# Cross-attention by token class and a mixture-of-experts layer on one core: the second norm's use and the scatter one round later, the front and routing pass one in another order, and unused small products on PE

## The chip, the cores and the metric

The kernel runs on one core of one Trainium2 chip. The metric is the device time of one execution in microseconds (us). Engines: PE (TensorE, matrix products), DVE (VectorE), ACT (ScalarE), POOL (GpSimd), and SP (SyncE), which issues DMAs.

## What is computed

The input x has 2048 tokens of 512 float32 features. The reference, cut to what matters:

```python
# first layer: each token belongs to one of 4 classes by its id; ctx is (4, 512, 512)
h = layernorm(x)
y = (silu(h @ ctx[e].T) * (h @ ctx[e].T)) @ ctx[e].T      # e = class of the token
x = x + y
# second layer
g = layernorm(x); n = rmsnorm(g) * norm_w
scores = softmax(n @ gate_w.T)                            # 32 experts, the 4 best per token, weights normed
routed = sum over the 4: weight * ((silu(n @ w13[e][:, :256]) * (n @ w13[e][:, 256:])) @ w2[e])
shared = (silu(n @ sg) * (n @ su)) @ sd
out = x + g + routed + shared
```

## The kernel before, in words

All large products are done in three parts: each float32 operand is split in a high part (rounded to fp32r, by ACT) and a low part (the difference, by DVE), and PE adds high x high, high x low and low x high (`three_products`, lines 221 to 223). Work goes by tiles of 128 tokens.

**First stage (`context`).** Tokens are sorted by class with a table made of one-hot products; here they fill 18 tiles, each of one class. One class's matrix (`ctx`, 512 x 512) is split by `high(e)` on ACT (line 476) and `low(e)` on DVE (line 536, about 2.3 us each). Each engine then runs a software pipeline written by hand: `pipeline` takes a list of parts with skews, and in round i it emits the parts in the order of the list, part p for tile i - skew(p). Rounds 0 to 11 are unrolled, with the tile's number known, then follows a loop. The order in the list is the order in the engine's queue, so a wait holds up all that stands behind it. The parts of a tile:

- POOL `gather` (skew 0, line 374): indirect DMA of the tile's rows of x; `rstd1` (2, lines 379, 381, 384): the first norm's scale and bias; `rstd2` (7, lines 391 to 398): those of the second norm (`affine`); `scatter` (9, line 406): indirect DMA of the results `hb` to `hb_dram`. Order: scatter, rstd1, rstd2, gather.
- DVE `stats1` (2, lines 612, 615): statistics of the rows; `x1` (7, lines 641, 644, 647): the residual sum and its statistics, which waits for base of the tile two before, as x1 has two buffers; `t1lo` (3, line 630), `t2lo` (5, line 634): low parts; `rows` (8, line 624): the scatter's index; `hn` (8, line 653); `weights` (0): low(1) in round 3, low(2) and low(3) in round 4, and pieces of the shared weights; `a` (4, line 627): the product with the gate.
- ACT `t1hi` (3, line 506), `t2hi` (5, line 510), `keep` (2, line 498), `weights` (0), `h` (2, line 515), `silu` (4, line 502), `x2` (7, line 520), `base` (8, line 525), in this order.
- PE `t1` (3) and `t2` (5), four transposes each (line 440); `g1` (4) and `g2` (6), twelve products each. Order: t1, t2, g1, g2.

h, a, x1, x2 and `hb` have two buffers. `rows`, `hn` and `base` of a tile wait until the scatter of the tile two before has landed. When all scatters have landed, POOL raises `stored`, and SP reads the first four tiles of the second stage (line 332).

**Second stage (`shared_routing_and_experts`).** Routing pass one goes over 8 pairs of tiles: PE transposes them (line 848), ACT and DVE split them (lines 977 and 1074), PE makes the logits (into `sps_gu`), ACT copies them (`lrow`, line 985), PE turns them back (`back`, line 864), DVE subtracts the maximum (`shift`, lines 1056, 1057), ACT takes exp (line 981), DVE finds the best (`top`, lines 1063 to 1066). On DVE round q is shift(q-2), t1lo of the pair q, top(q-3); on ACT it is t1hi of pair q, exp(q-2), lrow(q-1); on PE t1 of pair q, logits(q-1), back(q-2). SP refills the four row buffers (line 763). Then come the tables of the second sort (DVE, up to line 1213, which raises `listed`), beside the shared expert (PE, lines 221 to 223; POOL adds its results to `out`, line 800), and the experts: 80 tiles, gathered (lines 794, 822), run through PE and added to `out` by line 836, while the experts' weights stream in and are split (lines 1041 and 1253).

Of the kernel before, what the change touches and what calls it, by code (L numbers as in the profile page):

```python
# [22 lines left out]
ACT = mybir.ActivationFunctionType  # L23
AX = mybir.AxisListType

P = 128
# [3 lines left out]
G = TOKENS // P  # L30
# [23 lines left out]
RMS_EPS = 1e-6  # L54
W_SETS = 3
HL = C + CI


class Memory:
# [131 lines left out]
def number_of_quads(eng, entry):  # L191

    return eng.value_load(entry, min_val=0, max_val=MAX2 // RING - MIN_QUADS) + MIN_QUADS
# [11 lines left out]
def looked_up(eng, row, back, base, found):  # L205

    def look(pair):
        v = eng.value_load(row[:, bass.ds(pair, 1)], min_val=0, max_val=base ** (back + 1) - 1)
        for i in range(back + 1):
            found[i - back] = (v // base ** i) % base  # L210
    return look
# [7 lines left out]
def three_products(pe, acc, left_hi, left_lo, right_hi, right_lo, start, stop):  # L219

    pe.matmul(acc, left_hi, right_hi, start=start, stop=False)  # L221
    pe.matmul(acc, left_hi, right_lo, start=False, stop=False)  # L222
    return pe.matmul(acc, left_lo, right_hi, start=False, stop=stop)  # L223


def build(nc, m):
# [22 lines left out]
def context(nc, m):  # L249


    with ExitStack() as st:
# [82 lines left out]
        def _(pool):  # L335
# [71 lines left out]
                                            hb[:, t.par].rearrange("p a n -> p (a n)"), None,  # L407
                                            bounds_check=TOKENS - 1, oob_is_err=False).then_inc(hbs[t.par], 16)

            pipeline(pool, pairs, [("scatter", 9), ("rstd1", 2), ("rstd2", 7), ("gather", 0)], emit)  # L410
            m.carry(pool)
            count = number_of_pairs(pool, m.tab1[0:1, 1, 0:1], MAX1)
            for q in hbs:
# [3 lines left out]
        @block.tensor  # L417
        def _(pe):
            pe.wait_ge(m.s["consts"], 1)
            pe.wait_ge(m.s["counted"], 1)  # L420
            for g in range(G):
                mm = pe.matmul(ps_cnt, m.ones_b[:], M[:, g, :], start=(g == 0), stop=(g == G - 1))
            mm.then_inc(m.s["counts"], 1)
            pe.matmul(ps_rank, m.before_b[:], M[:].rearrange("p g e -> p (g e)"), start=True, stop=False, skip_group_check=True)
            for g in range(1, G):
                mm = pe.matmul(ps_rank[:, g * E1:], m.ones_b[:], M[:, 0:G - g].rearrange("p g e -> p (g e)"), start=False,
                               stop=(g == G - 1), skip_group_check=True)
            mm.then_inc(m.s["ranked"], 1)
            for i in range(G):
                pe.wait_ge(m.s["onehot"], i // C + 1)  # L430
                mm = pe.matmul(ps_list, hot[:, i, 0:P], hot[:, i, P:P + MAX1], start=(i == 0), stop=(i == G - 1))
            mm.then_inc(m.s["table"], 1)
            pe.wait_ge(m.s["listed"], 2)
            pairs = number_of_pairs(pe, m.tab1[0:1, 1, 0:1], MAX1)

            expert = {}

            def turn(dst, src):
                for c in range(C):
                    mm = pe.transpose(dst[:, c * P:(c + 1) * P], src[:, c * P:(c + 1) * P], m.ident[:])  # L440
                return mm

            def product(dst, hi, lo, t):
                e = bass.ds(expert[t.off], 1)
                for c in range(C):
                    mm = three_products(pe, dst[:], hi[:, t.par, c], lo[:, t.par, c], m.cth[:, e, c, :], m.ctl[:, e, c, :],
                                        c == 0, c == C - 1)
                return mm

            def emit(part, t):  # L450
                if part == "t1":
                    pe.wait_ge(s["h"], t.n + 1)
                    wait(pe, s["t1lo"], t.n)
                    turn(ps_t1, h[:, t.par]).then_inc(s["t1"], 1)
                elif part == "g1":
                    pe.wait_ge(m.s["ctx_split"], expert[t.off] + 1)
                    pe.wait_ge(s["t1lo"], t.n + 1)
                    wait(pe, s["a"], t.n)
                    product(ps_z, hth, htl, t).then_inc(s["g1"], 1)
                elif part == "t2":  # L460
                    pe.wait_ge(s["a"], t.n + 1)
                    wait(pe, s["t2lo"], t.n)
                    turn(ps_t2, a[:, t.par]).then_inc(s["t2"], 1)
                elif part == "g2":
                    pe.wait_ge(s["t2lo"], t.n + 1)
                    wait(pe, s["x1"], t.n - 1)
                    product(ps_y[t.par], ath, atl, t).then_inc(s["g2"], 1)

            pipeline(pe, pairs, [("t1", 3), ("t2", 5), ("g1", 4), ("g2", 6)], emit,
                     looked_up(pe, m.tab1[0:1, 0, :], BACK1, E1, expert))  # L470

        @block.scalar
        def _(act):
            def high(e):
                act.wait_ge(m.s[f"ctx_loaded{e}"], 16)
                nc.scalar.activation(m.cth[:, e], craw[:, e], ACT.Copy).then_inc(m.s["ctx_hi"], 1)

            high(0)
            act.wait_ge(m.s["gate_loaded"], 16)
            nc.scalar.activation(m.ghl[:, :, 0:E2], graw[:], ACT.Copy).then_inc(m.s["gate_hi"], 1)  # L480
# [44 lines left out]
                    nc.scalar.activation(hb[:, t.par, 1], x1[:, t.par], ACT.Identity, bias=affine[:, t.par, 1:2],  # L525
                                         scale=affine[:, t.par, 0:1]).then_inc(s["base"], 1)

            pipeline(act, pairs, [("t1hi", 3), ("t2hi", 5), ("keep", 2), ("weights", 0), ("h", 2), ("silu", 4), ("x2", 7), ("base", 8)], emit)

        @block.vector  # L530
        def _(dve):
# [63 lines left out]
            k(dve.tensor_scalar(tbf[:, 1, 0:1], row[0:1, 4, E1 - 1:E1], float(1 - 2 * MIN_PAIRS), None, ALU.add))  # L595
            k(dve.tensor_copy(m.tab1[:, 1, 0:1], tbf[:, 1, 0:1]))
            dve.tensor_scalar(m.tab1[:, 1, 0:1], m.tab1[:, 1, 0:1], 1, None, ALU.logical_shift_right).then_inc(m.s["listed"], 1)
            dve.wait_ge(m.s["listed"], 2)
            pairs = number_of_pairs(dve, m.tab1[0:1, 1, 0:1], MAX1)

            def emit(part, t):
                if part == "weights":
                    if isinstance(t.n, int):
                        for e in {3: (1,), 4: (2, 3)}.get(t.n, ()):
                            low(e)
                        if SHARED <= t.n < SHARED + HL // 2:
                            dve.wait_ge(m.s["sh_hi"], t.n - SHARED + 1)
                            dve.tensor_tensor(m.wl_s[:, piece(t.n)], sraw[:, piece(t.n)], m.wh_s[:, piece(t.n)].bitcast(F32),
                                              ALU.subtract).then_inc(m.s["sh_lo"], 1)
# [42 lines left out]
                    wait(dve, hbs[t.par], 16 * t.half)  # L652
                    dve.tensor_tensor(hb[:, t.par, 0], x2[:, t.par], m.normw[:], ALU.mult).then_inc(s["hn"], 1)

            pipeline(dve, pairs, [("stats1", 2), ("index", 0), ("x1", 7), ("t1lo", 3), ("t2lo", 5), ("rows", 8), ("hn", 8), ("weights", 0), ("a", 4)], emit)


def hots_of(i):
# [5 lines left out]
def shared_routing_and_experts(nc, m):  # L664


    with ExitStack() as st:
# [177 lines left out]
        def _(pe):  # L845
# [88 lines left out]

            pe.wait_ge(e["listed"], 1)
            pe.wait_ge(s["w_lo"], 2 * PIECES)
            quads = number_of_quads(pe, m.tab2[0:1, 2, 0:1])

            expert = {}
# [30 lines left out]

        @block.scalar
        def _(act):
            for q in range(G // 2 + 2):
                if q < G // 2:
                    for i in (2 * q, 2 * q + 1):
                        act.wait_ge(s["t1"], i + 1)
                        nc.scalar.activation(turned_hi(i).rearrange("p c n -> p (c n)"), turned[i % RING][:], ACT.Copy).then_inc(s["t1hi"], 1)
                if q >= 2:
                    act.wait_ge(s["shifted"], q - 1)
                    wait(act, s["top"], q - 3)  # L980
                    nc.scalar.activation(prob[:, q % 2], logits[:, q % 2], ACT.Exp).then_inc(s["exp"], 1)
                if 1 <= q <= G // 2:
                    act.wait_ge(s["logits"], q)
                    wait(act, s["back"], q - 2)
                    nc.scalar.activation(lraw[:, (q - 1) % 2], ps_gu[(q - 1) % 2][0:E2, 0:2 * P], ACT.Copy).then_inc(s["lrow"], 1)

            for i in range(G + 2):
                if i < G:
                    act.wait_ge(s["g1"], i + 1)
# [58 lines left out]
        def _(dve):  # L1048
# [5 lines left out]
            def shift(q):  # L1054
                dve.wait_ge(s["back"], q + 1)
                k_(dve.tensor_reduce(red[:, 2 * q:2 * q + 2], logit[q % 2], AX.X, ALU.max))
                dve.tensor_tensor(logits[:, q % 2], logit[q % 2], red[:, 2 * q:2 * q + 2].rearrange("p (j o) -> p j o", o=1).to_broadcast([P, 2, E2]),
                                  ALU.subtract).then_inc(s["shifted"], 1)

# [5 lines left out]
                dve.max_index(idx8[:, 2 * q, :], top8[:, 2 * q, :], prob[:, q % 2, 0])  # L1065
                dve.max_index(idx8[:, 2 * q + 1, :], top8[:, 2 * q + 1, :], prob[:, q % 2, 1]).then_inc(s["top"], 1)

            for q in range(G // 2 + 3):
                if 2 <= q < G // 2 + 2:
                    shift(q - 2)  # L1070
                if q < G // 2:
                    for i in (2 * q, 2 * q + 1):
                        dve.wait_ge(s["t1hi"], i + 1)
                        dve.tensor_tensor(turned_lo(i).rearrange("p c n -> p (c n)"), turned[i % RING][:],
                                          turned_hi(i).rearrange("p c n -> p (c n)").bitcast(F32), ALU.subtract).then_inc(s["t1lo"], 1)
                if q >= 3:
                    top(q - 3)
            dve.wait_ge(s["top"], G // 2)

            def low_a(i):  # L1080
# [203 lines left out]
```

## Time and profile before

| | us |
|---|---|
| median of 3 runs | 725.7 |
| lowest and highest run | 723.7, 728.16 |
| the profiled execution | 724.31 |
| its span, first to last instruction | 722.6 |
| PE busy in it | 629.1 (87%) |
| DVE, ACT, POOL busy | 440.7, 366.4, 339.4 |
| first stage, to the first read of the second | 0 to 184.6 |
| routing pass one, tables and shared expert, experts | to 221, to 304, to the end |

Times in the text are positions in the profiled execution, from the span's start. The time of an execution is a little longer than its span. Matrix products are pipelined on PE and the ends of the rows are modelled: the distance between two starts is the better measure of one. In brackets stands how long the engine was idle before a row and what released it; "issue" is time in which it waited for nothing that the profile shows. PEclk is the granted TensorE clock, 1.00 at full speed (2.4 GHz) and 0.50 at half (1.2 GHz).

### The profile page before, as it was taken

The numbers are of one execution on the slowest core, as the hardware profiler recorded it, in microseconds if no ns is written. First come the engines' busy times: TensorE is split into PE (matmuls) and PEld (weight loads), VectorE is DVE, ScalarE is ACT, GpSimd is POOL, SyncE is SP. The second block draws the span as 40 slices with busy tenths as digits, with TensorE's granted clock in tenths as the row PEclk, the third lists the DMA queues.
The fourth block names the chain that finished last, engine by engine and source line by source line (L and its number), as shares of the span: only waits on it lengthen the run. The fifth ranks groups of instructions, "written<-read, shape, count | busy, mean of one in ns | idle before, by whom it ended". The sixth has DMA issues, their size and how long they took to land.

```text
span 722.6 us, 15076 instructions
## 1 busy us (share of the span) xinstructions
PE 629.1 (87%) x3144; PEld 506.8 (70%) x3145; DVE 440.7 (61%) x1021; ACT 366.4 (51%) x635; POOL 339.4 (47%) x373
## 2 busy tenths in 40 slices
PE   2379998991579999889999999999999999999990
PEld 2268766771457788668887888788788788787870
DVE  7548666753268999745556556666554765655630
ACT  4357656542332422245566556666554665656530
POOL 2536676644000111245445464745665475565532
PEclk9989999997699999999999999999999999999996
DMA  6511222212676465466878888998787897978555
GB/s 240 171 39 61 99 88 87 108 67 87 195 271 212 59 142 120 60 158 194 218 214 234 211 239 234 260 286 209 196 254 213 239 252 233 243 228 232 115 64 69
DMA packets 35789, 124.68 MB, mean 173 GB/s; under 512 B 4784, under 2 KB 5936, under 8 KB 31152
## 3 DMA queue, kind: packets, MB, share of 16 engines
q0 software_dynamic: 24256, 59.26, 37.6%
q1 hardware_dynamic: 11504, 65.09, 25.2%
q8 instruction: 12, 0.20, 0.1%
q14 instruction: 17, 0.14, 0.1%
HBM read 90.51 MB, written 39.06 MB: 179 GB/s over the span
## 4 chain that ended last, share of the span: by engine, by line
PE 41%; DMA 21%; issue 12%; POOL 9%; DVE 8%; ACT 4%; POOLq 2%; ACTq 1%; DVEq 1%; SPq 0%
DMA out<-r_oh,e_sidx 10%; PE sps_gu L221 7%; PE sps_gu L223 7%; PE sps_gu L222 7%; DMA out<-normw,e_sidx 4%; PE sps_t L221 3%; PE sps_t L223 3%; PE sps_t L222 2%; DMA out<-r_rank,e_sidx 2%; POOL hb_dram L406 2%; DMA raw<-in_experts_w 1%; DMA both<-in_x,gather 1%; POOL c_rs L394 1%; POOL c_rs L381 1%; PE sps_table L848 1%
## 5 line engine op out<-in xcount | busy, mean ns | idle before, releaser
L1253 DVE TENSOR_TENSOR wl<-raw,wh x87 | 105.8, 1226 | 54.9 <-ACT wh L1041 51.2
L221 PE MATMUL sps_gu<-wh,s_xth 128*128 x320 | 133.0, 416 | 3.2 <-DVE s_xtl L1236 3.1
L223 PE MATMUL sps_gu<-wh,s_xtl 128*128 x320 | 126.6, 396 | 0.0
L222 PE MATMUL sps_gu<-wl,s_xth 128*128 x320 | 125.7, 393 | 0.0
L836 POOL DMA_INDIRECT out<-r_oh,e_sidx x40 | 68.0, 1700 | 88.8 <-issue 65.4
L1041 ACT ACTIVATE wh<-raw x87 | 91.2, 1060 | 16.0 <-issue 8.1
L822 POOL DMA_INDIRECT both<-hb_dram,e_gidx x76 | 81.7, 1074 | 32.2 <-issue 18.0
L221 PEld LDWEIGHTS sps_gu<-wh,s_xth 128*128 128x128 f32 x320 | 60.6, 189 | 15.3 <-issue 5.1
L1016 ACT ACTIVATE both<-sps_gu 128x256 f32<-128x256 f32 x80 | 30.6, 383 | 78.0 <-PE sps_gu L223 77.8
L223 PEld LDWEIGHTS sps_gu<-wh,s_xtl 128*128 128x128 f32 x320 | 60.5, 189 | 13.8
L221 PE MATMUL sps_t<-wh,s_ath 128*128 x160 | 69.6, 435 | 0.4
L222 PEld LDWEIGHTS sps_gu<-wl,s_xth 128*128 128x128 f32 x320 | 60.8, 190 | 10.7
L800 POOL DMA_DIRECT2D out<-both x16 | 14.1, 882 | 110.3 <-ACT both L1004 110.3
L223 PE MATMUL sps_t<-wh,s_atl 128*128 x160 | 63.0, 394 | 0.0
L222 PE MATMUL sps_t<-wl,s_ath 128*128 x160 | 62.7, 392 | 0.0
L1233 DVE TENSOR_TENSOR both<-both,sps_gu 128x256 f32<-128x256 f32 x80 | 33.4, 417 | 43.1 <-ACT both L1016 42.1
L836 POOL DMA_INDIRECT out<-normw,e_sidx x20 | 36.7, 1833 | 35.2 <-DMA out<-r_oh,e_sidx 31.6
L1236 DVE TENSOR_TENSOR s_xtl<-sps_rank,s_xth 128x512 fp32r<-128x512 f32 x40 | 27.5, 687 | 32.1 <-ACT s_xth L1020 32.1
L836 POOL DMA_INDIRECT out<-r_rank,e_sidx x20 | 33.3, 1663 | 24.4 <-DMA out<-normw,e_sidx 9.4
L1028 ACT ACTIVATE r_oh<-sps_t,weight 128x512 f32<-128x512 f32 x40 | 27.4, 684 | 30.1 <-PE sps_t L223 19.3
L1236 DVE TENSOR_TENSOR s_xtl<-sps_cols,s_xth 128x512 fp32r<-128x512 f32 x40 | 27.6, 689 | 18.5 <-ACT s_xth L1020 18.5
L223 PEld LDWEIGHTS sps_t<-wh,s_atl 128*128 128x128 f32 x160 | 30.0, 188 | 6.8
(300 smaller groups left out, 1426.0 us busy)
## 6 DMA issues: line engine op xcount, KB each, us to landing
raw<-in_experts_w SPq DMA_DIRECT2D x32, 1536.0 KB, 7.8
craw<-in_ctx_w SPq DMA_DIRECT2D x4, 1024.0 KB, 7.6
both<-hb_dram SPq DMA_DIRECT2D x16, 256.0 KB, 3.3
out<-hb_dram SPq DMA_DIRECT2D x4, 1024.0 KB, 17.8
out<-both POOLq DMA_DIRECT2D x16, 256.0 KB, 4.2
both<-hb_dram,e_gidx POOLq DMA_INDIRECT x76, 5.4
out<-r_oh,e_sidx POOLq DMA_INDIRECT x40, 5.7
sraw<-in_sg SPq DMA_DIRECT2D x1, 512.0 KB, 5.3
```

Source lines behind the costliest of these rows:

```text
L221: pe.matmul(acc, left_hi, right_hi, start=start, stop=False)
L222: pe.matmul(acc, left_hi, right_lo, start=False, stop=False)
L223: return pe.matmul(acc, left_lo, right_hi, start=False, stop=stop)
L406: pool.indirect_dma_start(m.hb_dram, bass.IndirectOffsetOnAxis(ap=sidx[:, t.par:t.par + 1], axis=0), hb[:, t.par].rearrange("p a n -> p (a ...
L822: pool.indirect_dma_start(e_xg[:, t.ring], None, hn_rows, bass.IndirectOffsetOnAxis(ap=gidx[:, t.ring:t.ring + 1], axis=0)).then_inc(e_gx[ ...
L836: pool.indirect_dma_start(m.out, bass.IndirectOffsetOnAxis(ap=sidx[:, t.ring:t.ring + 1], axis=0), e_y[t.ring], None, compute_op=ALU.add). ...
L1016: nc.scalar.activation(a[:, t.par], ps_gu[t.par][:, 0:INNER], ACT.Silu).then_inc(e["sil"], 1)
L1028: nc.scalar.activation(e_y[t.ring], e_py[t.par][:], ACT.Copy, scale=m.weight2[:, bass.ds(t.n, 1)]).then_inc(e["y"], 1)
L1041: nc.scalar.activation(m.wh[:, bass.ds(x % W_SETS, 1), ROWS[part], :], m.raw[:, bass.ds(x % 2, 1), ROWS[part], :], ACT.Copy).then_inc(e["h ...
L1233: dve.tensor_tensor(a[:, t.par], a[:, t.par], ps_gu[t.par][:, INNER:D], ALU.mult).then_inc(e["a"], 1)
L1236: dve.tensor_tensor(e_xtl[:, t.par].rearrange("p c n -> p (c n)"), e_t1[t.par][:], e_xth[:, t.par].rearrange("p c n -> p (c n)").bitcast(F ...
L1253: dve.tensor_tensor(m.wl[:, w, ROWS[part], :], m.raw[:, bass.ds(x % 2, 1), ROWS[part], :], m.wh[:, w, ROWS[part], :].bitcast(F32), ALU.sub ...
```

## The change

In the first stage: the scatter goes from skew 9 to 10, base from 8 to 9, x2 from 7 to 8, rows and hn from 8 to 9; on ACT base and x2 stand first in the round. Low(1) runs before the pipeline starts, low(2) in round 3 (part `third`), low(3) in round 4. ACT computes a Silu of two columns before its first split. In routing pass one shift goes from q-2 to q-3 and top from q-3 to q-4 on DVE, exp from q-2 to q-3 on ACT and behind lrow; the subtraction of shift waits for the exp of two pairs before, and an Exp and a Silu of two columns stand ahead of the routing and of the shared expert. `keep_busy` issues 24 products of 128 x 128 bfloat16 whose result nobody reads: before t1 of tile 0 and of tile 1 (after the first statistics), at the end of the first stage after `stored`, and before the experts.

```diff
+WARM = 24
...
+def keep_busy(pe, m, acc, times):
+
+    for _ in range(times):
+        pe.matmul(acc[:, 0:P], m.ones_b[:], m.before_b[:], start=True, stop=True)
...
-            pipeline(pool, pairs, [("scatter", 9), ("rstd1", 2), ("rstd2", 7), ("gather", 0)], emit)
+            pipeline(pool, pairs, [("scatter", 10), ("rstd1", 2), ("rstd2", 7), ("gather", 0)], emit)
...
                 if part == "t1":
+                    if isinstance(t.n, int) and t.n <= 1:
+                        pe.wait_ge(s["mv1"], 1)
+                        keep_busy(pe, m, ps_z, WARM)
                     pe.wait_ge(s["h"], t.n + 1)
...
+            pe.wait_ge(m.s["stored"], 1)
+            keep_busy(pe, m, ps_z, WARM)
...
+            act.wait_ge(m.s["consts"], 2)
+            nc.scalar.activation(a[:, 0, 0:2], m.minus_half[:], ACT.Silu)
             high(0)
...
-            pipeline(act, pairs, [("t1hi", 3), ("t2hi", 5), ("keep", 2), ("weights", 0), ("h", 2), ("silu", 4), ("x2", 7), ("base", 8)], emit)
+            pipeline(act, pairs, [("base", 9), ("x2", 8), ("t1hi", 3), ("t2hi", 5), ("keep", 2), ("weights", 0), ("h", 2), ("silu", 4)], emit)
...
+            low(1)
             dve.wait_ge(m.s["listed"], 2)
...
-                if part == "weights":
+                if part == "third":
+                    if isinstance(t.n, int) and t.n == 3:
+                        low(2)
+                elif part == "weights":
                     if isinstance(t.n, int):
-                        for e in {3: (1,), 4: (2, 3)}.get(t.n, ()):
-                            low(e)
+                        if t.n == 4:
+                            low(3)
...
-            pipeline(dve, pairs, [("stats1", 2), ("index", 0), ("x1", 7), ("t1lo", 3), ("t2lo", 5), ("rows", 8), ("hn", 8), ("weights", 0), ("a", 4)], emit)
+            pipeline(dve, pairs, [("stats1", 2), ("index", 0), ("third", 0), ("x1", 7), ("t1lo", 3), ("t2lo", 5), ("rows", 9), ("hn", 9), ("weights", 0), ("a", 4)], emit)
...
             pe.wait_ge(s["w_lo"], 2 * PIECES)
+            keep_busy(pe, m, e_t1[0], WARM)
...
+            nc.scalar.activation(prob[:, 0, 0, 0:2], m.minus_half[:], ACT.Exp)
+            for q in range(G // 2 + 3):
...
+                if q >= 3:
+                    act.wait_ge(s["shifted"], q - 2)
+                    wait(act, s["top"], q - 4)
+                    nc.scalar.activation(prob[:, (q - 3) % 2], logits[:, (q - 3) % 2], ACT.Exp).then_inc(s["exp"], 1)
+
+            nc.scalar.activation(ath[:, 0, 0, 0:2], m.minus_half[:], ACT.Silu)
...
                 k_(dve.tensor_reduce(red[:, 2 * q:2 * q + 2], logit[q % 2], AX.X, ALU.max))
+                wait(dve, s["exp"], q - 1)
...
-            for q in range(G // 2 + 3):
-                if 2 <= q < G // 2 + 2:
-                    shift(q - 2)
+            for q in range(G // 2 + 4):
+                if 3 <= q < G // 2 + 3:
+                    shift(q - 3)
...
-                if q >= 3:
-                    top(q - 3)
+                if q >= 4:
+                    top(q - 4)
```

## Rows read from the trace of the kernel before

**Rows 1.** Windows of stages: stretch, us, busy per engine (x instructions), PEclk, DMA, GB/s
```profile
53.00:80.00 27.00, 26.61 (x139) 22.15 (x137) 21.02 (x40) 17.68 (x28) 18.52 (x38) 1.00 0.23 74
80.00:131.00 51.00, 46.51 (x218) 35.87 (x216) 34.09 (x76) 29.12 (x49) 35.61 (x68) 1.00 0.28 98
...
196.00:218.00 22.00, 16.25 (x126) 12.77 (x125) 13.17 (x55) 8.29 (x23) 0.00 (x0) 1.00 0.76 266
...
316.00:700.00 384.00, 379.45 (x1877) 308.48 (x1878) 226.47 (x479) 227.97 (x401) 211.85 (x151) 1.00 0.81 219
```

**Rows 2.** Timeline of PE, first stage: start us, busy us, line, operation, [idle before]
```profile
53.10 0.60 PE L440 MATMUL ps_t<-ident,c_h 128*128 128x128 f32 x4
...
78.56 0.60 PE L440 MATMUL ps_t<-ident,c_h 128*128 128x128 f32 x4
...
145.96 0.66 PE L440 MATMUL ps_t<-ident,c_h 128*128 128x128 f32 x4 [0.57 <-ACT c_h L515]
```

**Rows 3.** Timeline of POOL, one tile of the first stage
```profile
97.04 1.02 POOL L406 DMA_INDIRECT hb_dram<-c_hb,c_sidx  x1 [0.94 <-ACT c_hb L525]
...
102.50 1.10 POOL L374 DMA_INDIRECT both<-in_x,c_gidx  x1 [0.51 <-issue]
104.57 1.02 POOL L406 DMA_INDIRECT hb_dram<-c_hb,c_sidx  x1 [0.97 <-issue]
```

**Rows 4.** Timeline of ACT, the base activation of the same tile
```profile
102.75 0.80 ACT L525 ACTIVATE c_hb<-c_x,c_affine 128x512 f32<-128x512 f32 x1
```

**Rows 5.** Timeline of all engines, the first tiles of the first stage
```profile
23.74 1.04 POOL L374 DMA_INDIRECT both<-in_x,gather  x1 [1.66 <-ACT c_h L515]
...
30.16 0.69 DVE L612 BATCH_NORM_STATS2 c_stat<-both 128x6 f32<-128x512 f32 x1 [2.50 <-DMA both<-in_x,gather]
...
31.68 4.48 DVE L536 TENSOR_TENSOR ctl<-craw,cth 128x2048 fp32r<-128x2048 f32 x2
31.69 2.70 POOL L381 TENSOR_TENSOR c_rs<-c_rs,minus_half 128x1 f32<-128x1 f32 x1
...
34.59 1.70 POOL L384 TENSOR_SCALAR c_rs<-c_mv,c_rs 128x1 f32<-128x1 f32 x1 [0.21 <-POOL c_rs L381]
...
37.16 1.28 ACT L502 ACT_TABLE_LOAD   x1
...
39.83 1.12 PE L440 MATMUL ps_t<-ident,c_a 128*128 128x128 f32 x4 [1.97 <-DVE c_a L627]
```

**Rows 6.** Timelines of DVE, POOL and SP, the end of the first stage
```profile
173.06 0.69 DVE L641 TENSOR_TENSOR c_x<-c_xr,ps_y 128x512 f32<-128x512 f32 x1 [3.63 <-ACT c_hb L525]
...
177.40 0.15 DVE L624 COPY c_sidx<-scatter 128x1 int32 x1 [1.64 <-DMA hb_dram<-c_hb,c_sidx]
...
181.19 0.96 POOL L406 DMA_INDIRECT hb_dram<-c_hb,c_sidx  x1 [0.31 <-issue]
...
184.64 1.75 SPq L332 DMA_DIRECT2D both<-hb_dram  x4
```

**Rows 7.** Chain of waits, routing pass one: start us, us, what
```profile
200.25 1.21 DVE s_xtl L1074 x2
...
203.10 0.25 PE sps_table L864 x2
...
203.85 1.21 DVE s_xtl L1074 x2
```

**Rows 8.** Timeline of PE, routing: eight transposes, and fifteen small products
```profile
199.66 1.09 PE L848 MATMUL sps_t<-ident,both 128*128 128x128 f32 x8
...
225.80 1.80 PE L914 MATMUL sps_rank<-r_m,ones_b 128*128 128x480 bf16 x15
```

**Rows 9.** Timeline of all engines, entry of the experts
```profile
305.96 1.00 POOL L794 DMA_INDIRECT both<-hb_dram,gather  x1 [0.30 <-issue]
...
311.99 1.30 POOL L794 DMA_INDIRECT both<-hb_dram,gather  x1 [2.73 <-DMA out<-both]
...
315.99 0.66 PE L848 MATMUL sps_cols<-ident,both 128*128 128x128 f32 x4 [0.21 <-DMA both<-hb_dram,gather]
```

More of the change, by code:

```diff
@@ L972, in _ @@
         def _(act):
-            for q in range(G // 2 + 2):
+            nc.scalar.activation(prob[:, 0, 0, 0:2], m.minus_half[:], ACT.Exp)
+            for q in range(G // 2 + 3):
                 if q < G // 2:
@@ L977, in _ @@
                         nc.scalar.activation(turned_hi(i).rearrange("p c n -> p (c n)"), turned[i % RING][:], ACT.Copy).then_inc(s["t1hi"], 1)
[L978 to L981, printed above, removed]
                 if 1 <= q <= G // 2:
```

## The prediction, made before the changed kernel had run

> **What bounds the kernel now.** I read the windows by stage first, then the timeline of each engine inside the stage that the change touches, and last the chain of waits.
>
> The windows show four kinds of stretch [rows 1]. The experts' stage (316 to 700) keeps PE busy 379.5 of 384 us and nothing in the diff changes its work, so it only moves. In the first stage PE is full from 53 to 80 (26.6 of 27 us) but not from 80 to 131 (46.5 of 51). In routing pass one (196 to 218) PE is busy 16.3 of 22 us and DVE 13.2: neither is full, so a dependence sets the pace.
>
> First stage. A tile costs 6.37 us while PE sets the pace (the transposes t1 of tiles 4 and 8 start at 53.10 and 78.56, four tiles apart) and 7.49 us from there on (tile 17 at 145.96, nine tiles later) [rows 2]. POOL shows why. One round there is the scatter's issue, the three small operations of rstd1, those of rstd2 and the gather's issue: from 97.04 to the end of the gather at 103.60, 6.56 us without a wait on another engine. Then 0.97 us pass before the next scatter [rows 3], and the base activation that it waits for ended at 103.55 [rows 4]. Base is emitted after x2, x2 waits for this same round's rstd2, and silu and with it t2 on PE stand behind h, which waits for rstd1. So scatter, rstd2, x2, base, scatter is a closed ring of one tile, with POOL, ACT and PE in it.
>
> Its end: x1 of the last tile starts at 173.06, the index of the last scatter waits 1.64 us for an earlier scatter to land, the last scatter is issued at 181.19 and SP starts the next reads at 184.64, 3.4 us later [rows 6]. That last x1 waited 3.63 us for base on ACT, not for a product.
>
> Routing pass one is a ring of 3.60 us per pair: DVE's two t1lo (from 200.25), PE's logits and back (end 203.35), DVE's shift, and t1lo again at 203.85 [rows 7].
>
> **Front.** Low(1) moves ahead of the first tile, low(2) to round 3, low(3) stays in round 4, and a two-column Silu draws the table load forward. Before, low(2) and low(3) ran as one block of 4.48 us from 31.68, and POOL's rstd1 of tile 2 needed 2.70 and 1.70 us in it; ACT then loaded the table (1.28 us) ahead of silu(0), and t2(0) came at 39.83 [rows 5]. After: low(1) delays the first statistics by 0.6 us; low(2) can fall on rstd1 of tile 0 and hold h(0) back about 2.5 us. I take that at nothing, because gather 2, issued at 23.74 behind h(0), reached DVE only at 30.16 [rows 5], twice the 3.4 us of rows 6: it queued with other loads, and going 2.5 us later it lands about as it did. Then low(3) alone, from about 31.8 to 34.1, leaves h(2) near 35.8 instead of 37.1, which was 34.59 + 1.70 + 0.8 (1.3 us), and the absent table load gives 1.3 more: t2(0) near 37.15, gain 2.7 us. Bounds: 0 if gather 2 lands 2.5 us later, 5.4 if PE's clock also stays up there.
>
> The Trainium skill (SBUF — State Buffer, section "SBUF: two separate sides") says that VectorE with two SBUF inputs and GpSimd exclude each other on a shared port pair for a whole instruction. The trace agrees: 2.70 and 1.70 us end with the two halves of that 4.48 us [rows 5]. By that rule alone low(2) in round 3 costs the 2.5 us above, which would leave 0.2 us of gain here.
>
> **Later scatter, x2 and base.** Nothing is computed more; each tile's x2, base, hn and scatter come one round later, base and x2 stand first in ACT's round. A scatter then finds its base ready, and the issue gap falls from 0.97 to the 0.30 us between indirect issues that wait for nothing (start 305.96) [rows 9]. POOL's round becomes 6.56 + 0.30 = 6.86 us, PE's stays 6.37. From the round of the first scatter, eight rounds hold all four parts; POOL falls behind 0.49 in each, 3.9 us, from about 0.5. It may be some 2.4 us late before silu and so t2 come late on PE: 2.0 us are lost. So nine tiles take 9 x 6.37 + 2.0 = 59.3 instead of 67.4 us, and t1(17) goes from 145.96 to 137.9. Bounds for the nine: 57.3 (PE alone) and 67.8 (gap still 0.97, no gain).
>
> From t1(17) PE has a full round (6.4), one without t1 (6.0), one of t2 and half the products (3.2), half the products (2.8): 156.3. X1(17) waits for base(15), which waits for scatter(13) to land; I allow 2.6 us (0 to 4): 158.9 instead of 173.06. From the last x1 to the reads it was 184.64 - 173.06 = 11.6 us [rows 6]. Now scatter(15) comes behind rstd2(17) on POOL, and hn(17) and base(17) wait until it lands, so 1.1 us more (0 to 3): 12.7, and the reads go at 171.6. Gain of loop and end: 13.0 us. What is queued behind the waits: on ACT base now stands ahead of t1hi, t2hi, h and silu, and waits for scatter(i-11) to land; with 3.4 us landing in a 6.4 us round it has landed.
>
> **Routing pass one.** Shift and top move one pair later on DVE, and ACT's lrow goes ahead of exp. DVE no longer waits for this pair's back before t1lo, so the ring opens. PE then needs eight transposes, about 1.0 (start 199.66) [rows 8], and logits with back, 203.35 - 201.46 = 1.89 [rows 7]: 2.9 us, above DVE's some 2.5 (two t1lo 1.21, shift 0.5, top 0.7). Six rounds at 0.7: 4.3 us, and 0.6 at the ends, since lrow(7) no longer stands behind exp(6) and the first transposes may run at the full clock: 4.9 us (2.5 to 6.5; loads of rows two pairs ahead, landing in 3.4 us, would need a round below 2). The Exp load falls where ACT waits anyway: 0.
>
> **Small products on PE.** 24 each: twice ahead of the first transposes, after "stored", before the experts. Fifteen of them with 256 columns on average (15 blocks of 32 down to one) took 1.80 us, 0.12 each [rows 8]; at 128 columns 0.06, at half clock 0.12: 1.4 or 2.9 us for 24. Bounds 0.03 and 0.22 each, 0.8 to 5.2 us: the latter by a transpose's 0.11 at full clock [rows 8], doubled. The Trainium skill (TensorE: Matmul & The Clock Gate, section "Wait — 56ns, not 53.3ns?") gives 55.6 and 106.7 ns for 128 columns; by it, as an estimate, 24 take 1.3 or 2.6 us; no row here has this form. First place: from 21.1 to 24.0, while h(0) is awaited; second, while h(1) is. Third: 2.9 us under the reads' landing, taken at the scatter's 3.4 us (at 5.2 they would cost 1.8). Fourth: 1.4 us before gather 0 arrives; what could be won is the half-clock g1(0), but t1(2) waits in PE's order for gather 2, issued at 311.99 after the last adds to out, and starts at 315.99 [rows 9]. So 0 (0 to 1.6 gained). I take all four at 0.
>
> **Sum.** 2.7 + 13.0 + 4.9 = 20.6 us off the profiled execution's 724.3 (span 722.6): **703.7 us**. That execution lies 1.4 us under the median of 725.7, within the runs shown (723.7 to 728.2).
>
> **Rivals.**
> A. POOL becomes the bound: the gap stays near 0.97 or more stalls of its small operations beside DVE appear. For it: the 0.51 us ahead of a gather whose waits were met [rows 3]. Against: 0.30 in rows 9. With rounds of 7.2, nine take 64.8: 709 us. Chance 0.18.
> B. The products hold PE's clock in the front: g1(1), which ran at half clock after 39.83, gets 2.7 us faster: 701 us. Against: no product is added between 31 and 37 us, where PE has nothing. Chance 0.12.
> C. The front gives nothing, as low(2) holds h(0) and gather 2 lands as much later, or the third set outlasts the landing: 706.5 to 708 us. Chance 0.12.
> D. Slower: a scatter's landing enters the ring. Its buffer ring is landing L, base 0.8, x1 and statistics 1.9, rstd2 2.1, gather 1.6, issue 0.5, for two tiles: 2 rounds = L + 6.9. Thirteen rounds lose the 20.6 us once a round is 8.0, so from L = 9.1; at L = 12 a round is 9.45 and the kernel takes 744 us. Against: L was 3.4, and DMA is busy 0.28 there [rows 1, 6]. Chance 0.03.
> The forecast keeps 0.55, with its own range 699 to 707.5.
>
> **How the numbers follow.** The likeliest case is 703.7. Low end: 20.6 with 2 more of front, 1.5 of routing and 3 of the loop, 697. High end: A and C together, 711. A measurement here tells about 1%, 7 us, from no change. Faster by over 1% holds in all but D and a failed opening of both rings: 0.95; same 0.02; slower 0.03.
>
> **What would show it.** T1 on PE at 6.4 to 6.6 us per tile to the end; scatters without a wait for L525; the first read of stage two near 169 (all less 2.7); pairs at 2.9 us; L1041 and the rest unchanged. Wrong if t1's spacing stays at 7.2 or more, if ACT waits for scatters, or if the pairs stay above 3.3.

## The result, and the profile after

The changed kernel takes 701.16 us (median of 4 runs, 698.52 to 702.91) against 725.91 us (4 runs, 723.7 to 728.16): a ratio of 0.9656, with a 95% interval of 0.9609 to 0.9703. The profiled execution took 702.91 us with a span of 701.2 us. Against the 724.31 us from which the prediction counts that is 21.4 us less; 20.6 were forecast. In the run e2 below, one of the four times (719.94 us) fell in a slower state of the chip, and its ratio leaves it out.

The windows by stage come first, with the columns of [rows 1]. The stretches are the same stages, shifted with the work, but not of the same length.

```profile
50.00:76.00 26.00, 26.00 (x133) 21.78 (x132) 20.71 (x39) 18.45 (x29) 18.01 (x38) 1.00 0.20 62
76.00:133.00 57.00, 56.95 (x286) 47.55 (x285) 43.91 (x94) 39.41 (x63) 41.72 (x89) 1.00 0.31 109
175.00:193.00 18.00, 18.00 (x148) 15.24 (x146) 13.23 (x44) 10.47 (x24) 0.00 (x0) 1.00 0.75 245
294.00:692.00 398.00, 384.68 (x1894) 311.11 (x1892) 225.87 (x482) 229.97 (x405) 216.45 (x155) 0.99 0.80 212
```

PE is full in the second half of the first stage (56.95 of 57 us; it was 46.5 of 51) and in routing pass one (18.00 of 18; it was 16.3 of 22). Both rings are open. The last stretch reaches 14 us further into the experts' stage than its counterpart in [rows 1]; over 294 to 678, 384 us as there, PE is busy 378.65 us (it was 379.45).

Next the timeline of PE, the transposes of tiles 4, 8 and 17, which answer to [rows 2]:

```profile
50.22 0.60 PE L447 MATMUL ps_t<-ident,c_h 128*128 128x128 f32 x4
...
75.69 0.60 PE L447 MATMUL ps_t<-ident,c_h 128*128 128x128 f32 x4
...
133.26 0.60 PE L447 MATMUL ps_t<-ident,c_h 128*128 128x128 f32 x4
```

From tile 8 to 17 it is 57.57 us, 6.40 a tile, where it was 67.40. The timeline of POOL gives the reason, and answers to [rows 3]:

```profile
102.08 1.02 POOL L413 DMA_INDIRECT hb_dram<-c_hb,c_sidx  x1 [0.30 <-issue]
...
107.40 1.09 POOL L381 DMA_INDIRECT both<-in_x,c_gidx  x1 [0.51 <-issue]
108.80 1.02 POOL L413 DMA_INDIRECT hb_dram<-c_hb,c_sidx  x1 [0.30 <-issue]
```

The scatter waits 0.30 us instead of 0.97. A round is 6.72 us here; over three rounds (102.08 to 122.40) it is 6.77. Over the eight rounds that hold all four parts it is 6.69, since the first three took 6.38, 6.77 and 6.39:

```profile
68.88 1.02 POOL L413 DMA_INDIRECT hb_dram<-c_hb,c_sidx  x1 [0.30 <-issue]
...
122.40 1.02 POOL L413 DMA_INDIRECT hb_dram<-c_hb,c_sidx  x1 [0.30 <-issue]
```

The end of the first stage, timelines of ACT, DVE, POOL and SP (it answers to [rows 6]):

```profile
154.13 0.81 ACT L539 ACTIVATE c_hb<-c_x,c_affine 128x512 f32<-128x512 f32 x1 [3.15 <-DMA hb_dram<-c_hb,c_sidx]
...
155.25 0.69 DVE L659 TENSOR_TENSOR c_x<-c_xr,ps_y 128x512 f32<-128x512 f32 x1 [3.01 <-ACT c_hb L539]
...
160.11 1.07 POOL L413 DMA_INDIRECT hb_dram<-c_hb,c_sidx  x1 [0.34 <-issue]
...
163.65 0.81 ACT L539 ACTIVATE c_hb<-c_x,c_affine 128x512 f32<-128x512 f32 x1 [3.03 <-DMA hb_dram<-c_hb,c_sidx]
...
165.52 0.96 POOL L413 DMA_INDIRECT hb_dram<-c_hb,c_sidx  x1 [3.07 <-DVE c_hb L671]
...
168.84 1.76 SPq L339 DMA_DIRECT2D both<-hb_dram  x4
```

Here the new order does wait for scatters to land: base(15) 3.15 us, and x1(17) behind it 3.01 us; base(17) 3.03 us for the scatter issued at 160.11 (3.54 us from issue to base). Before these, ACT waits for a landing only once, 1.67 us ahead of base(14) at 148.45, which also lies behind the last t1. The reads go at 168.84 instead of 184.64.

The ledger of landmarks, in us of each span; gains are running totals:

| landmark | before | after | gain |
|---|---|---|---|
| t1(4) on PE | 53.10 | 50.22 | 2.9 |
| t1(17) on PE | 145.96 | 133.26 | 12.7 |
| first read of stage two | 184.64 | 168.84 | 15.8 |
| cast of the expert numbers (routing) | 221.04 | 197.85 | 23.2 |
| t1(2) of the experts | 315.99 | 292.72 | 23.3 |
| last scatter-add issued | 713.79 | 692.46 | 21.3 |

### The profile page after: what moved, and what is told of

Its sections match the earlier page's. It is cut to its first block, busy times and chain, and to the rows that moved or that the text cites. A ratio compares the mean times of both kernels' runs of the same rounds, so it can differ in the third digit from the quotient of the medians.

```text
span 701.2 us, 15255 instructions
## 1 busy us (share of the span) xinstructions
PE 628.1 (90%) x3239; PEld 510.7 (73%) x3241; DVE 439.6 (63%) x1019; ACT 368.2 (53%) x637; POOL 333.8 (48%) x373
## 4 chain that ended last, share of the span: by engine, by line
PE 50%; DMA 20%; issue 10%; DVE 8%; POOL 6%; POOLq 2%; ACT 2%; DVEq 1%; ACTq 0%; SPq 0%
PE sps_gu L222 8%; PE sps_gu L224 7%; PE sps_gu L223 7%; DMA out<-r_oh,e_sidx 6%; DMA out<-r_rank,e_sidx 5%; DMA out<-normw,e_sidx 4%; PE sps_t L222 3%; PE sps_t L224 3%; PE sps_t L223 3%; PE sps_rank L866 2%; PE ps_z L222 2%; PE ps_z L224 2%; PE ps_z L223 2%; DMA raw<-in_experts_w 1%; PE sps_table L866 1%
## 5 line engine op out<-in xcount | busy, mean ns | idle before, releaser
L840 POOL DMA_INDIRECT both<-hb_dram,e_gidx x76 | 84.1, 1106 | 31.7 <-issue 17.4
L854 POOL DMA_INDIRECT out<-normw,e_sidx x20 | 34.9, 1744 | 31.8 <-DMA out<-r_oh,e_sidx 28.1
L854 POOL DMA_INDIRECT out<-r_rank,e_sidx x20 | 31.6, 1581 | 22.8 <-DVE e_gidx L1248 9.5
```

Of the source, the lines that this page charges most:

```text
L840: pool.indirect_dma_start(e_xg[:, t.ring], None, hn_rows, bass.IndirectOffsetOnAxis(ap=gidx[:, t.ring:t.ring + 1], axis=0)).then_inc(e_gx[ ...
L854: pool.indirect_dma_start(m.out, bass.IndirectOffsetOnAxis(ap=sidx[:, t.ring:t.ring + 1], axis=0), e_y[t.ring], None, compute_op=ALU.add). ...
```

## The experiments

Ten kernels ran, in three sets; each set shared one chip with runs of the kernel before. Ratios are to those.

**e1_skews_back** undoes the later scatter, base and x2, and their place in ACT's order.

```diff
-pipeline(pool, ... [("scatter", 10), ...
+pipeline(pool, ... [("scatter", 9), ...
-pipeline(act, ... [("base", 9), ("x2", 8), ("t1hi", 3), ... ("silu", 4)]
+pipeline(act, ... [("t1hi", 3), ... ("silu", 4), ("x2", 7), ("base", 8)]
-("rows", 9), ("hn", 9)
+("rows", 8), ("hn", 8)
```

> The changed kernel with the old skews and ACT's old order (scatter 9, x2 7, base 8, rows and hn 8, base and x2 last), all else of the change kept. Theory (the ring scatter, rstd2, x2, base, scatter set 7.5 us per tile): t1 on PE is again 7.5 us apart from tile 8 or 9 to tile 17, nine tiles take about 67 instead of 57.6 us, a scatter again starts about 0.95 us behind the gather with a wait for base, and the reads of stage two go at about 181.8 (before's 184.64 less the 2.9 of the front); the kernel takes about 13 us more than the changed one, about 714. Rival (the other edits of the first stage, above all the front, feed the loop): t1 stays below 6.8 us and less than 6 us are lost.

Measured: 714.71 us, ratio 0.9819 (0.9776 to 0.9861). The nine tiles take 67.55 us again, and from t1(17) to the reads it is 38.68 us, to the hundredth what it was before. The reads come 13.35 us after those of the changed kernel. Its timeline of ACT and POOL shows the ring closed again:

```profile
107.86 0.80 ACT L539 ACTIVATE c_hb<-c_x,c_affine 128x512 f32<-128x512 f32 x1
...
109.65 1.02 POOL L413 DMA_INDIRECT hb_dram<-c_hb,c_sidx  x1 [0.96 <-ACT c_hb L539]
```

**e2_routing_back** undoes the order of pass one.

```diff
-for q in range(G // 2 + 4):
-    if 3 <= q < G // 2 + 3:
-        shift(q - 3)
+for q in range(G // 2 + 3):
+    if 2 <= q < G // 2 + 2:
+        shift(q - 2)
...
-    if q >= 4:
-        top(q - 4)
+    if q >= 3:
+        top(q - 3)
```

On ACT, exp stands ahead of lrow again, and the subtraction of shift no longer waits for exp.

> The changed kernel with routing pass one in the old order on DVE and ACT, the early Exp and Silu kept. Theory (the ring t1lo, logits, back, shift, t1lo): pairs 3.6 us apart again in place of 2.67, the start of the sort (the first cast of the expert numbers) 6 to 7.4 us later against the first read, kernel about 7 us above the changed one, 708. Rival (the faster pass came from the full clock or from the table load at the start): pairs at 2.7 to 3.0 us and less than 3 us lost.

Measured: 709.38 us, ratio 0.9741 (0.9681 to 0.9801). Timeline of PE, "back" of three pairs in this kernel and then in the changed one:

```profile
182.80 0.30 PE L882 MATMUL sps_cols<-ident,both 32*128 32x32 f32 x2
186.41 0.30 PE L882 MATMUL sps_table<-ident,both 32*128 32x32 f32 x2
190.02 0.30 PE L882 MATMUL sps_cols<-ident,both 32*128 32x32 f32 x2
```

```profile
179.53 0.30 PE L882 MATMUL sps_table<-ident,both 32*128 32x32 f32 x2
...
182.21 0.30 PE L882 MATMUL sps_cols<-ident,both 32*128 32x32 f32 x2
...
184.88 0.30 PE L882 MATMUL sps_table<-ident,both 32*128 32x32 f32 x2
```

3.61 us a pair against 2.67. From the reads to the cast it is 35.72 us here, 29.01 in the changed kernel and 36.40 before. The part of that ahead of the first back does not depend on the order: it takes 10.48 us here, 11.18 before, and 10.4 to 11.9 in the kernels with the new order. From the first back to the cast it is 25.24 us here and 25.22 before, against 18.32 in the changed kernel: 6.9 us belong to the order.

**e3_no_products** drops all four sets of products, whose results nothing reads (WARM = 0).

> The changed kernel with none of the unused products (the waits ahead of them kept). Theory (they lie beside waits): g1(1), which the trace of the changed kernel shows ended before t1(3) at 42.66, runs at half clock again and takes up to 2.7 us longer, if the first two sets had any effect at all; the third and fourth set are worth 0 to 0.7 us; first read of stage two 0 to 2.7 us later. Theory A (products worth nothing): all landmarks within 0.5 us of the changed kernel's, 701. Theory B (they hold the clock): t1(3) at 45 instead of 42.66 and g1(0) of the experts 1.6 us longer, of which none reaches the end since t1(2) waits for its gather anyway; 702 to 704.

Measured: 704.02 us, ratio 0.9657 (0.9603 to 0.9712), the ratio of the changed kernel. T1(3) comes at 42.43 against 42.66, and the reads at 168.50. From the reads to the cast it was 29.85 against 29.01 us, which looked like 0.8 us for the third set; the repeat below takes that back.

**e4_front_back** puts low(1), low(2) and low(3) back to rounds 3 and 4 and takes the early Silu out.

```diff
-act.wait_ge(m.s["consts"], 2)
-nc.scalar.activation(a[:, 0, 0:2], m.minus_half[:], ACT.Silu)
...
-low(1)
...
-if t.n == 4:
-    low(3)
+for e in {3: (1,), 4: (2, 3)}.get(t.n, ()):
+    low(e)
```

> The changed kernel with low(1), low(2), low(3) where they stood and without the early Silu. Theory (front worth 2.7 us: 1.3 by low(3) alone and 1.3 by the table load): t2(0) near 39.8 in place of 37.73, t1(4) near 53 in place of 50.22, everything behind it later by the same 2 to 3 us; kernel about 704. Rival (the clock carries the gain): t1(4) stays within 1 us of 50.22 as the products are still there.

Measured: 703.77 us, ratio 0.9651 (0.9605 to 0.9697). T1(4) comes at 52.82, 2.60 us later than in the changed kernel, and the reads 2.57 us later. The front is worth that, though the totals alone can't tell it.

**e5_low_back** does the same with the early Silu kept (one run).

> The changed kernel with low(1), low(2), low(3) where they stood, the early Silu kept. The undone front cost 2.6 us at t1 of tile 4 (52.82 against 50.22). Theory (half of it is the table load of 1.28 us ahead of silu(0), half the 4.48 us block on DVE): t1(4) near 51.5, t2(0) near 38.8. Rival (only the block counts, since ACT loads while it waits anyway): t1(4) near 52.8.

Measured: 701.41 us; t2(0) at 38.54 and t1(4) at 50.98. Of the 2.60 us the table load holds 1.84 and the moves of low 0.76. Programs with the same front place t1(4) anywhere from 49.66 to 50.80, so the second share is barely more than chance.

**e6_old_order_new_skews** keeps the later rounds but leaves x2 and base at the end of ACT's round (one run).

```diff
-[("base", 9), ("x2", 8), ("t1hi", 3), ("t2hi", 5), ("keep", 2), ("weights", 0), ("h", 2), ("silu", 4)]
+[("t1hi", 3), ("t2hi", 5), ("keep", 2), ("weights", 0), ("h", 2), ("silu", 4), ("x2", 8), ("base", 9)]
```

> The changed kernel with the new skews but ACT's old order within a round (t1hi, t2hi, keep, weights, h, silu, x2, base). Theory (the order opens the ring, not the lateness: now x1(i-7) on DVE waits in its round for base(i-9), which stands behind silu(i-4) and so behind PE's g1 of the same round, and a(i-4) stands behind x1 on DVE): a new ring silu, x2, base, x1, t1lo, t2lo, hn, a, t2 of about 10 us per tile from the tenth round on; 745 to 760 us, slower than the kernel before. Rival (one round of lateness is what counts): 6.4 to 6.9 us per tile and 701 to 705 us.

Measured: 779.57 us, 53 us more than the kernel before on the same chip (726.37). Its timeline of DVE:

```profile
117.87 0.69 DVE L659 TENSOR_TENSOR c_x<-c_xr,ps_y 128x512 f32<-128x512 f32 x1 [6.21 <-ACT c_hb L539]
...
130.41 0.69 DVE L659 TENSOR_TENSOR c_x<-c_xr,ps_y 128x512 f32<-128x512 f32 x1 [7.21 <-ACT c_hb L539]
```

X1 writes over what base reads, and base(i-9) now ends the round in which x1(i-7) is emitted: DVE waits for ACT's whole round, PE for DVE, ACT for PE. A tile takes 12.5 us between these two rows, and 11.9 on average over the nine. The place in ACT's order is not a detail of the change; the later rounds alone lose far more than they gain. The ring was foreseen, but 745 to 760 us were expected: its round was set too short, perhaps because PE also slows down in it: four transposes of a take 1.11 us instead of 0.60, and the granted clock is 0.74 from 115 to 128. That is argued, not tested.

**e7_x2_at_once** has base first but x2 in its old round and place (one run).

```diff
-[("base", 9), ("x2", 8), ("t1hi", 3), ...
+[("base", 9), ("t1hi", 3), ... ("silu", 4), ("x2", 7)]
```

> The changed kernel with x2 back in its old place (skew 7, last in ACT's round) and base alone first in the round at skew 9, scatter 10, rows and hn 9. Theory (the scatter's wait for base closed the ring; x2 behind rstd2 is harmless as POOL does not wait for it in that round): 6.4 to 6.9 us per tile, reads within 2 us of 168.8, 701 to 704 us. Rival (x2's wait for rstd2 holds up t1hi and with it PE): more than 7.0 us per tile, 707 us or more.

Measured: 702.81 us. The loop is as fast (57.0 us for the nine tiles): the late x2 is not needed for it. From t1(17) to the reads it is 39.6 us, though, against 35.6. Without t1 and silu as cover, x2 waits 4 to 5 us for its own round's rstd2, and base and x1 stand behind it:

```profile
155.82 0.81 ACT L534 ACTIVATE both<-c_x,c_affine,c_rs 128x512 f32<-128x512 f32 x1 [4.57 <-POOL c_affine L405]
...
157.64 0.69 DVE L659 TENSOR_TENSOR c_x<-c_xr,ps_y 128x512 f32<-128x512 f32 x1 [3.38 <-ACT c_hb L539]
```

That x1 is the last one; in the changed kernel it starts at 155.25, 2.4 us earlier. So x2's extra round pays in the stage's end.

**e8_low3_later** takes low(3) in round 5. (This serves only inputs whose first pair is not of expert 3, as here.)

```diff
-if t.n == 4:
+if t.n == 5:
     low(3)
```

> The changed kernel with low(3) in round 5 in place of round 4. Theory (low(3) from 32.44 holds rstd1 of tile 2 for 2.70 us in place of 0.57, which is on the path): h(2) 2.1 us earlier, t1(2) near 34.4 in place of 36.52, t1(4) near 48.1 in place of 50.22, and all behind it earlier by 2 us: about 699. Rival (the next block holds rstd1(3) or a(1) as long, or PE's half clock takes it back): t1(4) within 0.7 us of 50.22.

Measured: 699.12 us, ratio 0.9605 (0.9539 to 0.967). Timeline of DVE and POOL, first the changed kernel, then this one:

```profile
32.44 2.28 DVE L550 TENSOR_TENSOR ctl<-craw,cth 128x2048 fp32r<-128x2048 f32 x1
32.45 2.70 POOL L388 TENSOR_TENSOR c_rs<-c_rs,minus_half 128x1 f32<-128x1 f32 x1
```

```profile
32.47 0.56 POOL L388 TENSOR_TENSOR c_rs<-c_rs,minus_half 128x1 f32<-128x1 f32 x1
...
37.58 2.28 DVE L550 TENSOR_TENSOR ctl<-craw,cth 128x2048 fp32r<-128x2048 f32 x1
37.75 2.24 POOL L391 TENSOR_SCALAR c_rs<-c_mv,c_rs 128x1 f32<-128x1 f32 x1 [0.21 <-POOL c_rs L388]
```

The block is gone from tile 2, whose t1 comes 2.1 us earlier, and sits on tile 3: of the 2.1 us, 0.8 are left at t1(4) (49.44) and 1.0 at the reads. About 2 were expected at both. E10, with the same move, has t1(4) at 50.00, inside the spread of the unmoved front. E8 has the lowest median of all, but its interval overlaps that of the changed kernel, so a faster version is not shown.

**e9_same_again** is the changed kernel unedited.

> The changed kernel once more, nothing edited, to see how much one program differs between its own executions in the two stretches that the sums leave open. Theory A (the 1.9 us by which the experts stage of the changed kernel was longer than before, 399.74 against 397.80 us from the first turn of its third tile to the last scatter-add, is chance): this time between 397 and 400.5 and not tied to the version, reads near 168.8, cast of the expert numbers near 197.9, last scatter-add 690 to 692.5, time 700 to 702. Theory B (the change itself lengthens that stage): again 399.5 to 400.5 from that turn to the last scatter-add.

Measured: 701.1 us (5 runs), ratio 0.9658 (0.9626 to 0.9691). From t1(2) of the experts to the last scatter-add it is 397.47 us, against 399.74 in the first profile and 397.80 before. Theory A holds for that stage: those 1.9 us were chance. Routing is the surprise: 30.20 us from reads to cast, with the third set in place, more than e3's 29.85 without it. Timeline of PE, the first transposes of routing, in e9 and then in e3:

```profile
168.72 2.74 PE L230 MATMUL ps_z<-before_b,ones_b 128*128 128x128 bf16 x24 [16.96 <-POOLq L422]
172.08 1.97 PE L866 MATMUL sps_t<-ident,both 128*128 128x128 f32 x8 [0.61 <-DMA both<-hb_dram]
```

```profile
172.08 1.97 PE L866 MATMUL sps_t<-ident,both 128*128 128x128 f32 x8 [20.73 <-DMA both<-hb_dram]
```

Same start, same duration, with and without 24 products. The windows from 172.00 to 173.50, of the changed kernel's first profile and then of e9, have the granted clock behind the five engines:

```profile
172.00:173.50 1.50, 1.28 (x8) 0.84 (x8) 0.00 (x0) 1.40 (x3) 0.00 (x0) 1.00 0.89 269
```

```profile
172.00:173.50 1.50, 1.42 (x7) 1.43 (x8) 0.00 (x0) 1.49 (x3) 0.00 (x0) 0.50 0.74 266
```

It was 1.00 (2.4 GHz) in the one and 0.50 (1.2 GHz) in the other, in the same program; e3 has 0.50 as well.

**e10_third_set_only** leaves out the first, second and fourth set, with low(3) as in e8.

> Left out: the first, second and fourth set of 24 products, whose results nothing reads; the low part of expert 3's weights is taken one round later, as in the run before it. Theory A (only the third set pays, since the first two stand ahead of a wait for h and the fourth hides under gather 2): reads of the routing stage 167.8 give or take 0.5, from there to the cast of the expert numbers 29.0, as with all four sets, and the time 699 to 701, level with the changed kernel run beside it. Theory B (the sets work together, by keeping PE at full clock in the front and at the entry of the experts): the front is longer than in the changed kernel by 0.6 us or more at t1(4), or the experts' entry is later than 94.9 us after the cast, and the time is 702 or more.

Measured: 700.25 us, ratio 0.9653 (0.9613 to 0.9693). T1(4) at 50.00, reads at 168.66 (a little later than expected), 28.77 us to the cast, and 94.5 us from there to t1(2) of the experts (94.87 in the changed kernel). So the other three sets are worth nothing that shows, as theory A has it. That the third set pays is not shown: with it e9 took 30.20 us to the cast, and e3 without it 29.85. The first transposes of stage one, in this kernel and then in the changed one:

```profile
25.43 1.11 PE L447 MATMUL ps_t<-ident,c_h 128*128 128x128 f32 x4 [11.98 <-ACT c_h L528]
```

```profile
25.44 0.66 PE L447 MATMUL ps_t<-ident,c_h 128*128 128x128 f32 x4 [1.32 <-ACT c_h L529]
```

In this pair the four are faster behind the products; in four other kernels with the products they are not (last section). Either way t1(1) starts at 29.52 to 29.57, when h(1) is there, so nothing can come of it.

## Why the prediction was right, step by step

**Front (2.7 forecast, 2.9 measured), by two errors that cancel.** Both halves were there, the first one smaller. Low(2), 2.26 us from 22.15, did hold POOL's L391 for 1.93 us, and h(0) came at 24.57 instead of 22.11. Gather 2 followed it, 2.46 us later than in [rows 5], yet reached DVE at 30.92, only 0.76 later than 30.16. Timelines of DVE, POOL, ACT and PE, first one row of the kernel before, then the changed kernel:

```profile
22.11 0.81 ACT L515 ACTIVATE c_h<-both,c_rs 128x512 f32<-128x512 f32 x1 [0.18 <-POOL c_rs L384]
```

```profile
22.15 2.26 DVE L550 TENSOR_TENSOR ctl<-craw,cth 128x2048 fp32r<-128x2048 f32 x1
22.61 1.93 POOL L391 TENSOR_SCALAR c_rs<-c_mv,c_rs 128x1 f32<-128x1 f32 x1 [0.21 <-POOL c_rs L388]
24.57 0.81 ACT L529 ACTIVATE c_h<-both,c_rs 128x512 f32<-128x512 f32 x1 [2.65 <-POOL c_rs L391]
26.20 1.04 POOL L381 DMA_INDIRECT both<-in_x,gather  x1 [1.66 <-ACT c_h L529]
...
30.92 0.69 DVE L630 BATCH_NORM_STATS2 c_stat<-both 128x6 f32<-128x512 f32 x1 [3.47 <-DMA both<-in_x,gather]
...
37.73 0.66 PE L447 MATMUL ps_t<-ident,c_a 128*128 128x128 f32 x4 [0.55 <-DVE c_a L645]
```

That delay was the term taken at nothing, and it cost 0.76 us: h(2) came 0.67 us earlier instead of 1.3, and t2(0) at 37.73 instead of 37.15, a gain of 2.1 us there. The other 0.8 us came between t2(0) and t1(3), which took 4.93 us instead of 5.71, and the sum had nothing for it. The windows from 40 to 43, before, changed and e3, show a higher granted clock:

```profile
40.00:43.00 3.00, 3.00 (x10) 2.52 (x11) 1.82 (x4) 1.84 (x3) 1.01 (x3) 0.50 0.20 75
```

```profile
40.00:43.00 3.00, 3.00 (x13) 2.38 (x11) 0.00 (x0) 0.96 (x2) 1.17 (x2) 0.71 0.02 8
40.00:43.00 3.00, 3.00 (x14) 2.26 (x13) 0.49 (x1) 1.46 (x3) 1.19 (x2) 0.91 0.14 53
```

It is not the products' doing: e3, which has none, is the fastest there, with 4.41 us. The Trainium skill's rule on the shared port pair (SBUF — State Buffer, "SBUF: two separate sides") was thus right on the operation (1.93 us beside the block, 0.27 alone), and the time it would have given for the front was not. The absent table load was worth more than its row: e4 and e5 differ by 1.54 us at t2(0), 1.28 being the load. The Trainium skill (ScalarE: Activation LUTs, "What ACT_TABLE_LOAD costs") adds 1.38 us of drain to a load of 1.28; in the trace before, the load starts 0.02 us after the end of h(2) and silu 0.01 us after the load, so no drain is seen there.

**Loop and end (13.0 forecast, 12.9 measured), by two errors that cancel.** The nine tiles took 57.57 us, not 59.3. The step that failed is the 2.0 us lost when POOL falls behind. Over the eight rounds it fell behind 2.6 us (53.52 from 68.88 to 122.40, against 8 x 6.37), not 3.9, as only the later rounds were 0.4 us longer than PE's. With the start 0.5 us late and the 2.4 us of slack that the prediction allowed, 0.7 would have been lost; 0.27 reached PE, at tile 17. The end took 35.58 us from t1(17) to the reads, not 33.7. I had the right wait and the wrong size: x1(17) came 21.99 us after t1(17), not 21.0 (3.6 us behind the end of PE's last product at 151.6, for which I allowed 2.6; in 3.01 of them DVE was idle), and from there 13.59 us, not 12.7, since base(17) waits 3.03 us for the scatter that stands behind rstd2(17). E1 undoes both parts, 9.98 and 3.10 us.

**Routing (4.9 forecast, 7.4 measured).** Two sizes were off. A pair takes 2.67 us, not 2.9: I read logits with back as 1.89 us from the closed ring [rows 7], where PE started from idle and the first product took 0.30 us. Back to back, by the chain of waits, it is twelve products in 1.41 us and a back of 0.23, 1.64 together, beside 1.03 for the transposes. Five rounds from 3.61 to 2.67 give 4.7. The last two intervals between backs shrank too, from 3.61 and 1.43 to 1.77 and 0.53, 2.7 us, as the last pairs have no transposes ahead of them; I had 0.7 and 0.6 for that. The cast came 0.5 us later behind the last back (2.65 us, it was 2.15), and the stretch ahead of the first back was 0.5 us shorter here. The latter changes between executions: in e9, the same program, it was 0.7 us longer than before, and the gain of routing only 6.2.

**Small products (0 forecast).** 24 took 1.50 to 2.77 us, 0.063 to 0.115 each with the end of the last, about half of the upper bound drawn from [rows 8] at most; two starts lie 0.06 us apart in the sets of 1.5 us and 0.11 in those of 2.7. After the fourth set g1(0) ran at full speed (0.39 us a product), and t1(2) still waited 1.66 us for gather 2, as foreseen. E3, e9 and e10 show no gain and no loss that can be told from the spread between executions.

**Rivals.** A (POOL bound) is out: 0.30, not 0.97, though the 0.51 to 0.56 us ahead of gathers stayed. B: the first transposes ran at full speed (0.66 us for four), but t1(3) was not earlier than without products. The higher clock behind t2(0) was there, worth 0.8 us and not 2.7, and it came without them too. C is out by e4 for the front, and the third set ended at 171.56, 0.57 us before the first rows had landed. D: the landing, 3.5 us, entered only the stage's end. The ring that makes this change slower is another than D: e6's, in which ACT's order, not the landing, closes it.

**The rest.** The parts give 2.9 + 12.9 + 7.4 = 23.2 us at the cast, where 20.6 were forecast. In the profiled execution 1.9 of that is missing again at the end of the experts' stage. In the eleven profiles outside e6, none of which changes anything behind that t1(2), the stretch from it on took from 396.6 to 400.4 us. So the forecast of the total was closer than its sum deserved: the medians differ by 24.8 us.

## What to carry to other kernels

When a stage is bound by a ring through several engines, put the late half of a tile's work one round later and first in its engine's order. Here the later round without the first place closed a worse ring through a buffer's reuse (779.57 us); the first place without the later round was not run. Price the drained end apart from the loop, since the waits that the loop hides stand open there. Take an engine's own rate from rows where it runs back to back, not from the ring that starved it, and compare landmarks near the edit, because totals of one program differ by more than a small edit is worth.

## What the runs showed that was not expected

- The clock of the same instructions in the same place differs between executions. After the first set of 24 products (always 2.74 us from 21.4), t1(0) at 25.44 took 0.66 us in some profiles (after, e8, e9) and 1.11 to 1.12 in others (e1, e2, e6, e7), and what runs up to there is the same in all of them. One profile does not show what unused products on PE bring. The granted clock doesn't tell the two apart here: it is 1.00 already from 21.40 to 24.20, over 24 products at 0.114 us each, as the window shows (PE's busy time is the first number behind the comma, the granted clock the third from the end):

```profile
21.40:24.20 2.80, 2.72 (x24) 2.45 (x24) 2.65 (x3) 0.52 (x1) 2.36 (x3) 1.00 0.51 128
```

- A POOL operation that falls into a DVE block ends behind the block, later by its own length less 0.14 us. Beside the 2.28 us from 32.44, L388 (0.57 us alone) ran 2.70 us from 32.45, 0.43 us beyond the block; beside the 2.26 us from 22.15, L391 (0.27 alone) ended 0.13 us beyond it, and so it did in e8 beside the block from 37.58.
- A gather issued 2.46 us later arrived only 0.76 us later. What it queued behind in the front was not tried apart.
